# A two-block transformer kernel whose list planner gets a third table of priorities

## The reference

```
x = x + attn_a0(layernorm(x))     # "full": 16 heads of 8, softmax over all 1024 keys
x = x + ffn0(layernorm(x))        # "ffn1": 128 -> 512 -> 128
x = x + attn_b0(layernorm(x))     # "causal" latent attention, then "local" (window 32), both with rope
x = x + ffn0(layernorm(x))        # "ffn2"
x = x + attn_a1(layernorm(x))     # "padded": local, 2 key heads
x = x + experts(layernorm(x))     # "moe1": 8 experts, top 2 of each token, 128 -> 352 -> 128
x = x + attn_b1(layernorm(x))     # "sink": window 128 and 4 sink tokens, 8 heads of 16
x = x + experts(layernorm(x))     # "moe2"
```

## Time and profile before

| | us |
|---|---|
| median of 3 runs | 2367.96 |
| lowest and highest of them | 2360.2, 2368.86 |
| span of the profiled execution | 2374.2 |
| PE busy in it | 2169.9 |
| DVE busy | 1642.4 |
| ACT busy | 1423.1 |
| POOL busy | 673.4 |

### The profile page before, as it was taken

The page is one execution under the profiler, slowest core; times in us unless marked ns, Lnnn a source line. Parts: engine busy times, 40 slices in busy tenths (PEclk is TensorE's granted clock), DMA queues, the critical chain, the costliest instruction groups (busy, mean ns, idle before and its releaser), DMA issues.

```text
span 2374.2 us, 62859 instructions
## 1 busy us (share of the span) xinstructions
PE 2169.9 (91%) x26187; PEld 1227.4 (52%) x26187; DVE 1642.4 (69%) x3685; ACT 1423.1 (60%) x2105; POOL 673.4 (28%) x602
## 2 busy tenths in 40 slices
PE   7788998889899999999999999999999989899997
PEld 3122232223223323334564566578777887677996
DVE  9898789998876475514453288476886876766665
ACT  1267756666787879998869755634444423344432
POOL 3400000012002001113224213445435544325563
PEclk9899999999999999999999999999999999999999
DMA  6700200101021012111322322636535673543786
GB/s 175 234 17 17 59 17 17 44 17 50 17 59 47 23 24 68 24 57 57 91 57 75 87 68 69 160 113 201 150 109 163 176 230 109 170 121 116 225 256 191
DMA packets 160746, 235.23 MB, mean 99 GB/s; under 512 B 21968, under 2 KB 81872, under 8 KB 160208
## 3 DMA queue, kind: packets, MB, share of 16 engines
q1 hardware_dynamic: 145456, 206.81, 31.6%
q0 software_dynamic: 9984, 20.73, 2.5%
q10 hardware_dynamic: 5024, 3.67, 0.6%
HBM read 156.28 MB, written 73.88 MB: 97 GB/s over the span
## 4 chain that ended last, share of the span: by engine, by line
PE 62%; ACT 12%; DVE 9%; issue 6%; DMA 6%; POOL 4%; SPq 2%; ACTq 0%; DVEq 0%; POOLq 0%
PE PS L1207 16%; ACT PT L1369 10%; PE PS L1187 9%; PE PS L1156 6%; PE PS L1256 6%; DVE MS L1611 5%; PE PS L1143 4%; PE PS L1273 3%; PE PS L1017 3%; PE PS L1056 2%; PE PS L1046 2%; PE PS L1217 2%; PE PS L1136 2%; POOL scr_y L1842 2%; PE PS L1067 1%
## 5 line engine op out<-in xcount | busy, mean ns | idle before, releaser
L1369 ACT ACTIVATE PT<-PS 128x1024 f32<-128x1024 f32 (+5 forms) x1200 | 1022.2, 914 | 415.9 <-PE PS L1187 406.0
L1611 DVE TENSOR_REDUCE MS<-PS 128x2 f32<-128x1024 f32 (+3 forms) x736 | 778.3, 1100 | 187.4 <-PE PS L1156 181.7
L1207 PE MATMUL PS<-PT,VA 128*9 128x512 f32 (+9 forms) x6720 | 560.2, 435 | 8.9 <-ACT PT L1369 8.5
L1187 PE MATMUL PS<-QO,KO 64*64 64x512 bf16 (+6 forms) x6240 | 422.1, 307 | 43.6 <-ACT PT L1369 27.5
L1187 PEld LDWEIGHTS PS<-QO,KO 64*64 64x64 bf16 (+1 forms) x6240 | 180.3, 106 | 277.9 <-ACT PT L1369 132.3
L1156 PE MATMUL PS<-KO,QO 61*64 61x512 bf16 (+2 forms) x3520 | 290.5, 330 | 32.7 <-DVE MS L1611 16.6
L1256 PE MATMUL PS<-SG,WB 128*128 128x128 f32 x2208 | 279.6, 280 | 12.1 <-DMA WB<-in_mW 9.2
L1256 PEld LDWEIGHTS PS<-SG,WB 128*128 128x128 f32 x2208 | 263.7, 195 | 20.7 <-DMA WB<-in_mW 11.0
L1156 PEld LDWEIGHTS PS<-KO,QO 61*64 61x64 bf16 (+1 forms) x3520 | 127.8, 105 | 257.5 <-DVE MS L1611 130.1
L1850 POOL DMA_INDIRECT scr_o<-SG,TO x184 | 181.0, 984 | 258.1 <-ACT SG L1404 222.3
L1207 PEld LDWEIGHTS PS<-PT,VA 128*9 128x9 f32 (+2 forms) x6720 | 125.2, 90 | 168.4 <-issue 111.9
(11 more groups left out here) (182 smaller groups left out, 2483.3 us busy)
## 6 DMA issues: line engine op xcount, KB each, us to landing
WB<-in_mW SPq DMA_DIRECT2D x184, 384.0 KB
PT<-scr_y SPq DMA_DIRECT2D x40, 264.0 KB, 4.6
PT<-scr_o SPq DMA_DIRECT2D x16, 512.0 KB, 5.5
QO<-scr_q_full SPq DMA_DIRECT2D x32, 192.0 KB
KO<-scr_k_full SPq DMA_DIRECT2D x32, 192.0 KB
QO<-scr_q_causal SPq DMA_DIRECT2D x32, 192.0 KB
QO<-scr_q_local SPq DMA_DIRECT2D x32, 192.0 KB
QO<-scr_q_padded SPq DMA_DIRECT2D x32, 192.0 KB
```

The costliest lines, as they stand in the source:

```text
L1187: p = mm(pb[c:c + n, h2, at:at + tn], k[:, k0 + c:k0 + c + n], q[:, t0:t0 + tn], start=not masked, stop=True, skip_group_check=masked)
L1207: p = mm(bank[32 * h:32 * h + D + 1, c0:c0 + tn], va[0:n, :], pt[0:n, plane, at:at + tn], start=s["first"] and j == 0, stop=s["last"] and ...
L1369: e = activation(pt[0:r, 0:n, a:b], ps[0:r, 0:n, a:b], ACT.Exp, scale=s["A"].scale)
L1611: v.tensor_reduce(to, got, AX.X, ALU.max).then_inc(S["top"], 1)
```

## The change

The steps, their buffers and the durations that the planner assumes are as they were. Added is a third table, `MORE`, with a number for each kind of step in each layer of each batch, which `add` sums into `lead`. All numbers of the two old tables are others, too, as are `SHORT` and `WORTH`. In the new source all lines behind `add` stand 93 lower: L1009 is L1102 there, L1156 is L1249, L1187 is L1280, L1207 is L1300.

```diff
-LEADS = dict(full=(121097, 70228, 71603, 22232), ffn1=(-39987, -13584, 141685, 197277), causal=(27622, -17639, 38536, -2778), local=(-92346, -32246, -33767, -11333), ffn2=(8451, 203535, 103159, 208081), padded=(101100, -24936, 10929, -11661), moe1=(-7069, -34020, -67110, -40081), sink=(85114, 2737, -27540, 1045), moe2=(-46108, -255154, 5755, -79333))
+LEADS = dict(full=(2323947, 154902, 252461, 55876), ffn1=(-547007, -2519135, -1116334, -168450), causal=(280504, -9418, 319458, -150177), local=(153230, -169994, -96852, -61844), ffn2=(409495, 1817258, -23600, 756035), padded=(497848, -14698, -70872, 59286), moe1=(15444, 561415, -2024453, -350444), sink=(1088845, 687357, 1261778, 596449), moe2=(-654180, 510133, 96146, 2109935))
...
-SHORT = dict(pe=705422039, act=1568, dve=1300, pool=419903, sp=18986641)
+MORE = {
...
+    "slot_load": dict(moe1=(-175553, -80169, -40052, 414111), moe2=(-361583, 536398, 216107, -970278)),
...
+    "top_full": dict(full=(279553, 94030, 420474, -57488)),
...
+}
+SHORT = dict(pe=451774124, act=1574, dve=1224, pool=7255526342059971584, sp=350446777)
...
-WORTH = 6210168
+WORTH = 9890825
...
+        if step.layer:
+            step.lead += 1000 * MORE.get(step.name, {}).get(step.layer[0], (0, 0, 0, 0))[step.layer[1]]
```

89 lines of the change are left out of this document (88 added, 1 removed).

## The result

The changed kernel takes 2337.86 us (median of 4 runs, 2329.1 to 2338.93) against 2368.41 for the kernel before in the same session (4 runs, 2360.2 to 2381.54): the medians are 30.6 us apart, 0.987. The ratio on record is 0.985 with a 95% interval of 0.9825 to 0.9875; it is not the quotient of these two medians, so I take the gain as 31 to 36 us. The forecast was 16 less, 2352; the time lies in its range, nearest to the case "more than that" (2336).

The account below looks back on a forecast made before the run. PE was taken to bound the kernel, with 281 us of idle time and empty matmuls movable. Terms 0 - 1 - 7 - 3 - 10 + 5 + 0 = -16 gave 2358.2 us in the span, 2352 as a median; range 2331 to 2379.

Parts of the forecast that it names:

- more than that: Rival: from 106 to 750 a quarter of 97 us idle and empty time goes; 2336 us, chance 0.17.
- The frame: Whole kernel: PE sets the time; its busy time without empty matmuls changes by no more than 10 us.
- Start to 527: To 106 us same list, 0 (-2 to +2); full attention of batches 0 and 2 to 527, -1 (-5 to +4).
- 527 to 750: First place shown: eleven of 16 places with empty matmuls and waiting go, half counted; -7 us (0 to -16).
- 750 to 1860: Batch 3's maxima spread over more of PE's list; a twentieth of 58.2 us idle, -3 us (-12 to +8).
- 1860 to 2040: Second place: transfer waits from SP's queue order and slow-clock stretches behind them shrink; -10 us (0 to -20).
- 2040 to 2190: Third place: sink attention of batches 1 and 3 loses expert steps as cover; +5 us (0 to +16).
- the slower case: Rival: uncovered sink attention of batches 1 and 3 waits up to 8 us at four chains; 2384 us, chance 0.13.
- 2190 to the end: Last experts, list nearly the same; 0 us (-3 to +4).
- Collisions of DVE and POOL: No fixed place: shared ports can make a tops chain 1.9 us late; counted as zero, +-4 in the range.
- The signs I named: PE idle near 10 us from 527 to 750, no PT<-scr_y wait above 1 us, clock above 0.93, sink idle about 8.

Follow-up runs that it names:

- before_no_empty: The kernel before without the empty matmuls behind the first 90 us of the planner's play, same order: 2369.99 us, 0.9985.
- token runs: The kernel before with three late token loads moved ahead in SP's queue, to batch 1's sink loads or the eighth tile's weights: 2374.38 us (1.0004) and 2372.89 (0.9997).
- after_no_ffn1: The kernel after with the third table left out for the steps of the first feed-forward block: 2359.71 us, 0.9946 of the kernel before.
- half maxima: The kernel before, same lists, each row maximum of the full attention reading 512 of its 1024 columns: 2356.27 us, 0.9925.
- half exponentials: The kernel before, same lists, the full attention's exponentials working on 512 of 1024 columns once each PT buffer has been written in full: 2345.22 us, 0.9887.
- tokens_ahead_b: The kernel before with three late groups of batch 0's tokens loaded just ahead of batch 1's first sink load in SP's queue: 2374.38 us, 1.0004.

## Why the prediction was right or wrong

**The frame held.** PE sets the time and its useful work stayed (2093.2 to 2087.4 us). The gain is idle time and empty matmuls. Counting the empty matmuls as slack was right: before_no_empty has 31 us less of time in which nothing but empty matmuls ran, and 29 us more idle time (233.3 for 204.4).

**Start to 527, forecast 0 and -1.** Measured -6 to 550 by this pair of profiles; the others of before's order have 545 to 550 there and those of after's 544 to 547, so about -3. The list differs from row 58 on, and from 58 to 80 us DVE is busy for 21.97 us in the new order against 16.96. By progress the new order is 5.5 us ahead at 80 and 6 at 550, so that this all lies where I had written that nothing should differ; from 106 to 527 there is next to nothing, as forecast. A small miss in size.

**527 to 750, forecast -7.** Right in mechanism as far as it went: PE idle 11.4 where I had written "near 10", empty matmuls x5 for x19. By progress the lead grows from 7.6 us at 527 to 18.3 at 750, so it is -11, inside the bounds.

**750 to 1860, forecast -3. This is the step that failed.** By progress the lead grows from 18.3 us at 750 to 37.2 at 1300 and is 36.2 at 1857: this term is -18, outside its bounds of -12 and +8, and all of it lies ahead of 1300. Of the middle part (550 to 1300), where -27 to -31 was measured, I had -7 and a share of this -3. I took a twentieth of 58.2 us idle, because the waits were short, and because the empty matmuls, which I used as the planner's own sign, did not fall there (33 and 32). But of the middle part's idle time three fifths waited for ACT (28.6 of 46.8 us), I had read ACT at 87%, and asked of the waits only whether they were long. They were 77, none over 1.2 us, and could be moved as well as a long one; the sum of waits that name `PT` fell to 15.7. And the place of the change that I showed, the maxima of batch 3 spread over more of the list, I had judged by DVE, where a quarter to a half of what the middle part brought hung on ACT's exponentials; what the rest hung on stays open. The middle part has the same work for PE with 17 us less for ACT in it, some 4 of which had been done before it and 9 were left for later (the rest is that ACT's instructions took 4 us less in all).

**1860 to 2040, forecast -10.** The size came out, the mechanism didn't. By progress the stretch is 1857 to 2050 before and 1820 to 2005 after, and the one behind it goes to 2194 and 2150. Before:

```profile
1857.00:2050.00 193.00, 170.66 (x1482) 148.15 (x1481) 141.32 (x403) 65.47 (x135) 92.39 (x87) 0.94 0.60 179
2050.00:2194.00 144.00, 140.73 (x1414) 107.16 (x1412) 104.59 (x331) 63.95 (x104) 58.86 (x58) 0.99 0.42 122
```

And after:

```profile
1820.00:2005.00 185.00, 166.93 (x1438) 147.04 (x1442) 145.70 (x413) 69.55 (x144) 96.62 (x92) 0.96 0.63 188
2005.00:2150.00 145.00, 141.46 (x1473) 107.23 (x1483) 100.91 (x319) 63.21 (x103) 50.20 (x48) 1.00 0.42 123
```

It takes 185 us for 193, idle 18.1 for 22.3, the granted clock 0.96 for 0.94. There is no wait for `PT<-scr_y` and none for `KO<-scr_k_sink`, as forecast, but 10.9 us for weights in place of 4.3: transfers' waits are 10.9 for 12.4. The token runs show that taking a wait out of the queue's head gives nothing by itself. The doubt that I wrote down ("one of the three may well turn up elsewhere") should have been the forecast of the term. The part of the term that did come is the clock: I had counted 5.7 us for two slow stretches gone, and in this stretch PE stood at half clock for 13.7 us where it had been 23.9, worth 5 at most. Why one of the slow stretches went while the transfers' waits stayed is not shown.

**2040 to 2190, forecast +5.** Measured +1: idle 3.5 for 3.3 and x7 empty matmuls, 2.2 us. The cover taken away was replaced by maxima of batch 3, as the argument against the slower case said; PE waited 1.2 us for `QO<-MTd` in all from 1820 to 2150. The slower rival is out. (Its bound of +16 was called a fifth of the stretch idle; 16 and the 3.3 already there are 13% of 150 us, a fifth would be +27.)

**2190 to the end, forecast 0.** Measured +6 in the pair of profiles, with 26.7 us idle for 22.7: a small miss, PE waiting there 6.9 us in six pieces for weights, where it had been 4.0, and 3.2 for the turn of a new layer. It lies outside the +4 of my bounds.

**The last part as a whole stays uncertain.** From 1300 on the two kernels' profiles differ by 0.5 us, those without empty matmuls by 3, those with cut maxima or exponentials by 9 to 15 in favour of the new order, though little is cut there. A shift in time of everything ahead changes which transfers and collisions meet; which ones was not tested.

**The rivals.** "More than that" has the right time, and by the wrong place: it took 24 us out of the slack from 106 to 750, where by progress 12 went; another 19 went from 750 to 1300. Collisions of DVE and POOL did what I had feared of them. `MTb<-MS` has a maximum of 0.457 us now, for 2.107, and one `MTb<-MTa` has 2.100, as one had before (2.099). But in the sink attention of the new order a small copy of DVE's stands ahead of an `MTb` chain, and ends only with the last of four instructions of POOL. Three lines out of that place:

```profile
1951.13 3.90 DVE L1646 COPY VA<-c_rest 128x8 f32<-128x8 f32 x1
...
1954.08 0.90 POOL L1926 TENSOR_TENSOR T<-PQ,c_rest 128x384 f32<-128x384 f32 x1
...
1955.82 0.34 PE L1257 MATMUL PS<-c_half,MTb 128*96 128x128 bf16 x1 [2.60 <-DVE MTb L1722]
```

The other three copies of this line took 0.16 to 0.85 us, and the longest of the four took 1.32 in the profile before. A copy of 3.9 us with PE's wait of 2.6 us behind it is in the profiles of all seven kernels that use the new tables throughout (after_no_ffn1 among them), and in none of the other thirteen. So it belongs to the new order, in the very stretch that I forecast at -10. That POOL held the copy is read from where both end (1955.03 and 1954.98); no run takes POOL's work away there.

**The signs I named.** PE idle near 10 us from 527 to 750, no wait for `PT<-scr_y`, the granted clock above 0.93 and PE's useful busy time unchanged all came out, and the time was still missed by as much as the forecast itself: none of these signs looked at 750 to 1300. The rise of idle time in the sink attention did not come, and the first 106 us did differ.

## What to carry to other kernels

Where a kernel's order comes out of a planner, read the planner's own end time first: it foretold each of seven orders within 0.7%, and this change as -29.8 us for a measured -30.6, where an estimate stretch by stretch gave -16. When no engine but one is full, add up the many short waits by the engine that they name, and look at the second engine's share over the same work; a hundred waits of a few tenths of a us are as movable as one long one. The name at a wait says where to look, and is no price: with less work for the engine named, a large part of the waits took the other's name. A wait at the head of a transfer queue is worth nothing by itself if the next transfer behind it is needed as soon: here it was handed on to the microsecond (12.4, 12.5, 12.3).

## What was not expected of the hardware

Taking out all empty matmuls after 90 us left the granted clock at 1.00 from 120 to 1140 and the time within 0.15%; in this kernel's dense part it is not they that hold up the clock. The Trainium skill ("TensorE: Matmul & The Clock Gate", section "HAM oscillation — how this bites in real kernels") tells of waits for transfers that let the clock fall. Here it also fell behind short waits for other engines. In the profile before it stood at half from 722.4 to 729.2 us, with waits of 0.30, 0.53 and 1.13 us for ACT ahead of that, and these are lines of PE's around its fall:

```profile
715.14 0.41 PE L1156 MATMUL PS<-KO,QO 61*64 61x512 bf16 x4
...
719.86 0.41 PE L1187 MATMUL PS<-QO,KO 64*64 64x512 bf16 x4 [0.53 <-ACT PT L1369]
721.40 0.41 PE L1187 MATMUL PS<-QO,KO 64*64 64x512 bf16 x4 [1.13 <-ACT PT L1369]
...
722.98 0.64 PE L1156 MATMUL PS<-KO,QO 61*64 61x512 bf16 x4
```

Four `top` matmuls take 0.64 us behind it, where they take 0.41 ahead of it. That the waits brought it down is the order of events, and was not tested. Such spells are rare here: all of those from 120 to 1140 add up to 13.7 us in the old order and 10.2 in the new one.

A difference of means can come from the clock alone. In the groups shown, `scores` take 392 ns as built, 387 with half maxima and 389 with half exponentials, which looks as if PE went faster when the engines beside it read less. But the window as built has 3.4 us at half clock and the other two have none, and tokens_ahead_b, with the same lists and full work up to there and no half clock either, has 390. The 1 to 3 ns that are left are not explained, and `top` goes the other way with half exponentials (396 for 394).
